# A state-space mixer whose decay-sum rows are loaded from ScalarE's queue instead of SyncE's

## The reference

```
proj = layernorm(x) @ in_proj_w.T            # gate, xBC, dt
xBC  = silu(causal_conv_4(xBC) + conv_b)     # -> hs (heads), Bm, Cm (per group)
dt   = softplus(dt + dt_bias);  cum = cumsum(dt * A)      # per head, along the sequence
y[i] = sum over j <= i of (C_i . B_j) * exp(cum_i - cum_j) * dt_j * hs_j  +  D * hs_i
g    = rmsnorm_per_group(y * silu(gate)) * norm_w
out  = x + g @ out_w.T
```

## Time and the profile before

| | us |
|---|---|
| median of 3 runs | 1973.42 |
| lowest, highest | 1969.29, 1976.84 |
| the profiled execution | 1968.67 |
| its span, first to last instruction | 1967.0 |
| mean granted TensorE clock | 0.969 of full speed |

### The profile page before, as it was taken

How to read it: one execution, slowest core, us unless ns; L and a number is a source line. 1 busy time by engine, 2 the same in 40 slices (tenths; PEclk the granted TensorE clock), 3 DMA queues, 4 the chain that set the end, 5 groups by cost and what they waited for, 6 DMA issues and landing times. The chain is left out here.

```text
span 1967.0 us, 32620 instructions
## 1 busy us (share of the span) xinstructions
PE 1827.2 (93%) x10772; PEld 1453.4 (74%) x10772; DVE 1367.9 (70%) x1722; ACT 1167.8 (59%) x2105; POOL 1420.5 (72%) x1424
## 2 busy tenths in 40 slices
PE   6998996669999999999999999999999999999967
PEld 4765775557887878778777878787888778877845
DVE  5654555586767876686768767866876686768755
ACT  3212433418775776677667757675776677677723
POOL 4313323527997999699869978996999699879854
PEclk9997998779999999999999999999999999999978
DMA  3000000023333334233333423333334233333301
GB/s 108 1 1 23 1 1 33 28 75 118 124 102 103 97 119 130 76 123 97 108 97 109 129 80 109 117 108 97 97 119 130 74 123 97 108 97 117 104 28 48
DMA packets 174814, 170.03 MB, mean 86 GB/s; under 512 B 11072, under 2 KB 142272, under 8 KB 174656
## 3 DMA queue, kind: packets, MB, share of 16 engines
q1 hardware_dynamic: 173696, 167.84, 27.6%
q10 hardware_dynamic: 960, 0.05, 0.0%
HBM read 165.22 MB, written 2.62 MB: 85 GB/s over the span
## 5 line engine op out<-in xcount | busy, mean ns | idle before, releaser
L142 PE MATMUL ps<-mix_xnT_hi,mix_w_hi 128*128 128x512 f32 x1152 | 463.8, 403 | 12.0 <-DVE mix_xT L1618 6.2
L144 PE MATMUL ps<-mix_xnT_hi,mix_w_lo 128*128 128x512 f32 x1152 | 455.9, 396 | 0.0
L143 PE MATMUL ps<-mix_xnT_lo,mix_w_hi 128*128 128x512 f32 x1152 | 455.6, 395 | 0.0
L1618 DVE SCALAR_TENSOR_TENSOR mix_xT<-ps,mix_cur,mix_xT 128x510 f32<-128x510 f32 x378 | 279.9, 746 | 139.2 <-ACT mix_xT L1485 130.3
L1436 POOL TENSOR_SCALAR_AFFINE_SELECT mix_spread<-mix_spread 128x256 f32<-128x256 f32 x512 | 316.7, 653 | 0.0
L1638 DVE TENSOR_TENSOR mix_decay<-mix_decay,mix_cb 128x1536 f32<-128x1536 f32 x128 | 300.2, 2382 | 4.5 <-ACT mix_decay L1511 4.5
L1534 ACT ACTIVATE mix_g_hi<-mix_gated 128x512 fp32r<-128x512 f32 x128 | 81.0, 633 | 316.0 <-POOL mix_gated L1413 284.0
L142 PEld LDWEIGHTS ps<-mix_xnT_hi,mix_w_hi 128*128 128x128 f32 x1152 | 217.9, 189 | 68.1 <-issue 12.5
L144 PEld LDWEIGHTS ps<-mix_xnT_hi,mix_w_lo 128*128 128x128 f32 x1152 | 217.7, 189 | 51.1
L1509 ACT ACTIVATE mix_decay<-mix_spread,mix_cur_ncum 128x256 f32<-128x256 f32 x512 | 253.8, 496 | 0.9 <-issue 0.6
L143 PEld LDWEIGHTS ps<-mix_xnT_lo,mix_w_hi 128*128 128x128 f32 x1152 | 218.1, 189 | 47.2
(11 more groups left out here) (257 smaller groups left out, 3397.7 us busy)
## 6 DMA issues: line engine op xcount, KB each, us to landing
mix_spread<-cum_rows SPq DMA_DIRECT2D x128, 512.0 KB, 3.8
mix_w_raw<-in_w_in_stream SPq DMA_DIRECT2D x144, 256.0 KB, 4.9
mix_spread<-cum_rows SPq DMA_DIRECT2D x128, 256.0 KB, 4.8
mix_wo_raw<-in_w_out_T SPq DMA_DIRECT2D x64, 256.0 KB, 4.9
att_w_raw<-in_w_attn_T SPq DMA_DIRECT2D x12, 256.0 KB, 4.2
x<-in_x SPq DMA_DIRECT2D x8, 256.0 KB, 4.5
ffn_w_raw<-in_w_ffn_T SPq DMA_DIRECT2D x2, 1024.0 KB, 6.5
out_rows<-x SPq DMA_DIRECT2D x8, 256.0 KB, 2.0
```

The costliest lines, as they stand in the source:

```text
L142: pe.matmul(out, lh, rh, start=(k == 0), stop=False)
L143: pe.matmul(out, lh, rl, start=False, stop=False)
L144: last = pe.matmul(out, ll, rh, start=False, stop=(k == tiles - 1))
L1618: dve.scalar_tensor_tensor(out=d[:, :, shift:T], in0=src[:, :, 0:T - shift], scalar=w[:, MK - 1 - shift:MK - shift], in1=d[:, :, shift:T], ...
```

## The change

`load_spread` becomes a function that takes the engine whose queue issues the transfers. SyncE issues only the two rows of the very first pair. For every later pair ScalarE issues them: head 0's row behind the previous pair's square and ahead of `scale_wo`, head 1's row behind `load_exp` and ahead of `high`. The wait for the exponentials moves with them. SyncE keeps the weights, in the same order among themselves.

```diff
+        def load_spread(engine, g, k, a):
+
+            head = GHEADS * g + 2 * k + a
+            at_least(engine, exped, head - 1)
+            row = cum_rows[bass.ds(head, 1), :].broadcast_to([P, ROWS]).rearrange("p (b t) -> p b t", t=T)
+            engine.dma_start(spread[:, a, :, 0:T], row).then_inc(spread_in[a], 16)
+            engine.dma_start(spread[:, a, :, T:BLK], row[:, :, P:T]).then_inc(spread_in[a], 16)
...
                 if first:
                     load_wo(g, 0)
-                    load_spread(g, 0, 0)
-                    load_spread(g, 0, 1)
+                    load_spread(sp, g, 0, 0)
+                    load_spread(sp, g, 0, 1)
...
                     if more:
                         load_wo(g, k + 1)
-                        load_spread(g, k + 1, 0)
                     for dg, j in mine[1:]:
                         load_w(LEAD + len(NEXT) * (g + dg) + j, LEAD + j)
-                    if more:
-                        load_spread(g, k + 1, 1)
...
                     elif not first:
                         square_pair(g - 1, PAIRS - 1, False)
+                    if has_next:
+                        load_spread(act, g, k + 1, 0)
                     scale_wo(g, k, first)
                     exps(g, k, 1, range(B))
...
                     if k < PAIRS - 1:
                         load_exp()
+                    if has_next:
+                        load_spread(act, g, k + 1, 1)
                     high(g, k, first)
```

More of the change, by code:

```diff
@@ L1341, in load_wo @@
                     .then_inc(wo_arrived[k % 2], 16)
[L1343 to L1349, removed]
             def body(g, first, last):
```

## The result

The changed kernel takes 2018.68 us at the median (2012.46 to 2021.47, 4 runs), the kernel before 1971.36 (1968.98 to 1976.84, 4 runs): ratio 1.0232, interval [1.0213, 1.0252]. That is 47 us slower, where no change was forecast (1974 us, 1965 to 1994). The profiled execution's span is 2015.1 us against 1967.0, 48.1 us more.

What follows compares the result with a forecast made beforehand. TensorE was taken to bound the mixer. 63 pairs at 0 us, plus about +1 us for the eight groups' k = 0, on the median of 1973.42 us gave 1974 us, range 1965 to 1994.

Steps and rivals of the forecast that it cites:

- What bounds the kernel: Mixer: TensorE sets its length, busy 182.0 of 185 us per group; changes elsewhere cost only what outlasts its cover.
- Part 1: SyncE's queue: weight loads no longer wait for the exponentials, but earlier weights are worth nothing, 0 us.
- Part 2: ScalarE's sequencer issues head 1's transfers at the gate product's end, 2.5 us later; head 0's at most 0.4 us later.
- Rival A: ScalarE's transfer leaves only when its datapath is through `load_exp`: +176 us, 2150 us; chance 0.10.
- The sum of the closed chain: Issue behind `load_exp`'s datapath makes a pair 23.8 us against 20.56; about 22 us a group, +176 us.
- Part 3: Pairs k = 1 to 7: gate 0.2 us late, 0.9 at worst against 1.8 us of cover: 0 us.
- rival B: k = 0's 3 us not caught up, TensorE waits in three or four pairs: 12 to 16 us, 1987 us; chance 0.22.
- Part 4: k = 0, once a group: gate 3.0 us late, 0.7 us spare before TensorE's product; cost 0, at the edge.
- C: Rows and weights on two queues, head 0's row lands earlier, GpSimd's short waits go: faster, 1966 us; chance 0.08.
- Rival U: Issuing on ScalarE's queue itself, or SyncE's lost order of rows and weights, costs: some half of the 47 us.
- V: Head 1's lateness adds up in all pairs; eight of 64 early give back an eighth: about 2012 us.

Runs made afterwards that it cites:

- m2: Changed kernel with the last C·B copies ahead of the convolution and the wait for head 1's row behind the gate's multiplications: 1959.69 us, ratio 0.9945.
- m1: Kernel before with the last C·B copies ahead of the convolution and the wait for head 1's row behind the gate's multiplications: 1962.05 us, ratio 0.9942.
- e6: Changed kernel with head 1's transfers ahead of `load_exp` instead of behind it: 2013.51 us, ratio 1.0209.
- e3: Changed kernel with head 1's row issued ahead of `silu_gate` in k = 0 alone: 1984.93 us, ratio 1.0059.
- e5: Changed kernel with GpSimd's wait for head 1's row moved behind the gate's two multiplications, ahead of the low parts: 1972.91 us, ratio 1.0007.
- e4: Changed kernel with VectorE's variance in k = 1 ahead of the convolution's first half instead of behind it: 1992.83 us, ratio 1.0102.
- e1: Changed kernel with only head 0's row on ScalarE's queue, head 1's from SyncE as before: 1975.65 us, ratio 1.0018.
- e7: Changed kernel with head 1's row issued from ScalarE's queue ahead of `silu_gate` in every pair: 1977.29 us, ratio 1.0024.
- e2: Changed kernel with only head 1's row on ScalarE's queue, head 0's from SyncE as before: 2004.6 us, ratio 1.0160.
- n8: Kernel before with VectorE's last two copies of C·B in k = 0 ahead of the convolution's first half: 1959.55 us, ratio 0.9935.

## Why the prediction was wrong

**What bounds the kernel**: right. TensorE sets the pace, and k = 4 to 7 kept it to the hundredth.

**Part 1**, SyncE's freed queue is worth nothing: right. The weights land 1.7 us sooner and nothing follows; m2 equals m1.

**Part 2**, when ScalarE issues: right. The reading by sequencer records gave the end of the gate product's second half; the row stands 0.14 us behind the activation that waits for it. Rival A is refuted by this and by e6. The sum of the closed chain, +176 us, did not come. Head 0's row goes out 0.4 us later than before, relative to the tap beside it, as forecast; the `issue` wait of 3.6 us in k = 0 that comes with it stood in no part of the prediction.

**Part 3**, k = 1 to 7: right for k = 4 to 7, whose cover of 1.8 us held, though the gate waits there 0.4 to 1.2 us on average where 0.2 was forecast. "The pairs k = 1 to 7 have the same distance between this sequencer record and the gate" was wrong for k = 1: its gate waits 2.4 us for the row, and in e3, with k = 0 on time, still 2.0. Wrong too for k = 2 and 3, with 0.67 and 0.54 us each, 8 us in all. There the cover was not that of k = 5: VectorE adds the rows to x ahead of the convolution (L1671 before, L1672 after), and TensorE already waited for it. I had put that into rival B and left it out of the sum. These rows show it for k = 3, VectorE before and then (in the next group) after, and TensorE's wait after:

```profile
1052.66 5.45 DVE L1671 SCALAR_TENSOR_TENSOR x<-mix_u,mix_rstd,x 128x512 f32<-128x512 f32 x4
```

```profile
1265.63 5.86 DVE L1672 SCALAR_TENSOR_TENSOR x<-mix_u,mix_rstd,x 128x512 f32<-128x512 f32 x4
...
1273.77 0.50 PE L142 MATMUL ps<-mix_xnT_hi,mix_w_hi 128*128 128x512 f32 x1 [0.67 <-DVE mix_xT L1619]
```

The four additions take 0.41 us longer, and TensorE's wait is 0.67 us where 0.3 was the longest. That they are stretched because GpSimd's low parts, shifted by the late gate, now run beside them is my reading; e5, which puts the gate back in time, brings k = 2 and 3 back, but no run has measured the two operations against each other.

**Part 4**, k = 0: here the prediction failed. Its first half was right, 3.0 us late by the sum and 3.27 measured. The step that failed is "The next pair's first convolution moves from 1197.17 to 1200.2, ends at 1202.5, and TensorE's product starts at 1203.21: 0.7 us spare." I followed the late convolution to the one consumer that I had in mind, the next product, and not to what else stands behind it on VectorE. Two instructions of 0.2 us for the variance stand there, and TensorE's output products wait for their banks some 3 us earlier than the product that I looked at. Before, these rows stood there, TensorE and then VectorE:

```profile
1198.63 1.84 PE L1806 MATMUL ps<-mix_ones,mix_squares 128*128 128x1 f32 x16
1200.34 0.48 PE L142 MATMUL ps<-mix_wo_hi,mix_g_hi 128*128 128x512 f32 x1
```

```profile
1199.62 0.16 DVE L1667 TENSOR_SCALAR mix_rstd<-ps 128x4 f32<-128x4 f32 x1
1200.51 0.16 DVE L1667 TENSOR_SCALAR mix_rstd<-ps 128x4 f32<-128x4 f32 x1 [0.73 <-PE ps L1806]
```

The convolution's first half ended at 1199.48 and the first variance takes 0.16 us, so for the output product at 1200.34 the cover was 0.7 us in all, and a delay of 3.0 us leaves 2.3 of it bare. In all seven groups the convolution comes 3.2 to 3.5 us later against the one-column products, and the output products 2.5 to 2.8: the difference is that cover of 0.7. e4 shows the place (k = 1 back at 22.35 with the gate just as late).

**The price of that step** has two halves. In one group in the middle (k = 1 of 27.39 us) the output products start 4.47 us behind the sums of squares instead of 1.71, 2.76 lost to the wait, and take 5.13 us instead of 2.87, 2.26 lost to the lower clock: 5.02 of the 5.04 us. The means of the seven groups are 2.6 and 2.1 us. Nothing in the prediction held a term for the clock.

```profile
1030.17 1.84 PE L1807 MATMUL ps<-mix_ones,mix_squares 128*128 128x1 f32 x16
1034.64 0.79 PE L142 MATMUL ps<-mix_wo_hi,mix_g_hi 128*128 128x512 f32 x1 [2.63 <-DVE mix_rstd L1668]
...
1039.77 0.40 PE L142 MATMUL ps<-mix_xnT_hi,mix_w_hi 128*128 128x512 f32 x1
```

**The rivals.** B named the right pairs, the right cause (k = 0's 3 us not caught up) and a price of 12 to 16 us, where 48 came; the waits that it had in mind, for the convolution in k = 2 and 3, made 8 of them, and the 33 of k = 1 went by the variance. C did not come. Rival U of the experiments fell with e1 and e7, but for some 3 us in k = 0, V with e3. The prediction's chances by outcome don't follow from those of its rivals either: the forecast, most of C and a third of B make some 0.73 for "same" and not 0.66.

**What stays open**: why head 0's later row, nearly harmless alone (e1), makes head 1's dearer by some 13 us. The profiles say that k = 1 goes from 26.47 (e2) to 27.12 and k = 2 and 3 from 0.23 and 0.09 above before to 0.67 and 0.54. In k = 0 the gate waits 3.05 us for head 1's row in e2 and 3.32 in the changed kernel, since its second transfer takes 4.6 us to land there and 4.9 here, and TensorE's wait for the variance grows by the same 0.3 us. Some 3 us of the 13 are the `issue` wait in k = 0. Why the transfer lands later, and why the `issue` wait grows, no run shows.

## What to carry to other kernels

When something comes late, follow it through each engine's program order and ask of every instruction queued behind it which bank or buffer it releases, and to whom; a 0.2 us instruction behind a late one can hold the engine that sets the pace. Put waits directly in front of the first use (e5), and put short instructions that free a bank of the busiest engine ahead of long ones (e4, n8): n8 gained 13 us on the kernel before by the pattern that the loss had shown. A cover measured in one iteration holds for the iterations with the same program; the odd ones (k = 0, 1, 2, 3 here) each need their own.

## What the runs showed of the hardware

ScalarE's sequencer issued a transfer ahead of its datapath, past two queued instructions (a table load of 1.28 us and an activation): 0.14 us behind the activation whose wait it had to pass, with the datapath 1.8 us behind. It did not pass an unsatisfied wait: in none of the groups g = 1 to 7 did head 1's row of k = 0 leave ahead of the second gate activation, which waited 2.20 us for TensorE in the group shown. In the kernel before, two address records with such a wait between them stand 3.1 us apart.

A stall of 2.3 to 2.6 us behind 16 one-column products went with a stretch at a granted clock of 0.62, and in another group, 1034 to 1040 us, of 0.54. This clock cost nearly as much as the stall itself: 1.6 us in the one group, 2.3 in the other. The same stall did not always have the same outcome. The stall of 1.8 us that each group has in k = 0 was followed by the lower clock in no group of the kernels before and changed, but in one group each of e1, e2, e4, e5 and e7, whose k = 0 took 33.5 to 34.3 us. In e3 and e4 it followed `issue` waits of 1.9 to 2.3 us, and in the changed kernel it did not follow those of 2.1 and 2.3.
